# Attention on one core: the causal mask of a diagonal piece added by one product over 128 rows in place of two over 64

## What is computed

```python
q = (x @ wq.T).reshape(B, S, N_HEADS, HEAD_DIM)      # B 4, S 2048, 16 heads of 16
k = (x @ wk.T).reshape(B, S, N_KV_HEADS, HEAD_DIM)   # 4 heads of keys and values
v = (x @ wv.T).reshape(B, S, N_KV_HEADS, HEAD_DIM)
attn = jnp.einsum('bqhd,bkhd->bhqk', q, k) * scale   # k, v repeated for 4 query heads each
causal = jnp.tril(jnp.ones((S, S), dtype=bool))
attn = jnp.where(causal, attn, jnp.float32(-jnp.inf))
attn = jax.nn.softmax(attn, axis=-1)
out = jnp.einsum('bhqk,bkhd->bqhd', attn, v).reshape(B, S, C)
```

## Time and profile before

| what | value |
|---|---|
| median of three executions | 8469.42 us |
| the three executions | 8474.6, 8468.7, 8469.42 us |
| span of the profiled execution, first to last instruction | 8471.3 us |
| TensorE busy in it | 7608.0 us, 90% of the span |
| VectorE busy | 7340.3 us, 87% |
| ScalarE busy | 5072.8 us, 60% |
| GpSimd busy | 3704.5 us, 44% |
| first and last mask product (both attentions) | 203.9 and 7929.3 us |

### The profile page before, as it was taken

One profiled execution on the slowest core, in us unless ns is written; L12 is line 12 of the kernel. 1 busy time (PEld: TensorE's weight loads), 2 busy tenths in 40 slices (PEclk: granted clock), 3 DMA queues, 4 the chain that ended last, 5 costly groups with the idle time before them and its releaser, 6 DMA issues. The chain is left out here.

```text
span 8471.3 us, 131822 instructions
## 1 busy us (share of the span) xinstructions
PE 7608.0 (90%) x38817; PEld 3068.7 (36%) x38818; DVE 7340.3 (87%) x10750; ACT 5072.8 (60%) x7665; POOL 3704.5 (44%) x1825
## 2 busy tenths in 40 slices
PE   6999999989987888888888888888889999999899
PEld 3333333325542333333333333333453333333355
DVE  6988888858877999999999999999658888888588
ACT  3577777762255666666665556556316777777622
POOL 0010011100016999999999999999400000110000
PEclk9899999989998999999999999999988999999999
DMA  6001101112262222222233333333561001010121
GB/s 177 18 19 20 19 19 19 20 37 70 67 232 91 85 83 83 84 83 83 83 98 103 100 100 100 101 103 97 164 181 18 19 19 19 19 22 18 36 78 61
DMA packets 531283, 603.88 MB, mean 71 GB/s; under 512 B 195488, under 2 KB 344736, under 8 KB 526560
## 3 DMA queue, kind: packets, MB, share of 16 engines
q1 hardware_dynamic: 526048, 562.63, 22.4%
q0 software_dynamic: 4608, 33.56, 2.0%
HBM read 397.75 MB, written 163.69 MB: 66 GB/s over the span
## 5 line engine op out<-in xcount | busy, mean ns | idle before, releaser
L833 DVE TENSOR_REDUCE ffn_att_mx<-psum 128x1 f32<-128x512 f32 (+3 forms) x4608 | 2728.0, 654 | 367.8 <-PE psum L674 209.2
L794 ACT ACTIVATE ffn_att_e<-psum,unscale 128x1024 f32<-128x1024 f32 (+3 forms) x2560 | 2376.5, 985 | 766.3 <-PE psum L739 760.3
L1707 POOL TENSOR_TENSOR scan_h<-scan_h,scan_cs 128x1024 f32<-128x1024 f32 x1024 | 2412.4, 2449 | 203.8 <-ACT scan_state L1878 198.0
L1788 PE MATMUL psum<-scan_h,ident 128*128 128x512 f32 x4096 | 1977.7, 624 | 158.9 <-POOL scan_h L1707 157.6
L2022 DVE TENSOR_TENSOR_SCAN scan_h<-psum,scan_state,scan_db 128x512 f32<-128x512 f32 x1408 | 1684.6, 1261 | 10.5 <-ACT psum L1920 10.5
L641 POOL TENSOR_SCALAR_AFFINE_SELECT ffn_att_e<-ffn_att_e 128x512 f32<-128x512 f32 x512 | 324.6, 634 | 3023.9 <-ACT ffn_att_e L794 3023.9
L674 PE MATMUL psum<-ffn_att_k,ffn_att_q 48*128 48x512 f16 (+3 forms) x5120 | 1438.8, 367 | 175.4 <-DMA ffn_att_v<-v 55.8
L1788 PEld LDWEIGHTS psum<-scan_h,ident 128*128 128x128 f32 x4096 | 777.7, 198 | 1321.1 <-issue 894.5
L705 PE MATMUL psum<-ffn_att_e,ffn_att_v 128*32 128x512 f32 (+3 forms) x10240 | 1240.4, 557 | 7.8 <-ACT ffn_att_o L809 2.4
L1920 ACT ACTIVATE psum<-scan_dt,scan_anr 128x512 f32<-128x512 f32 x1024 | 698.2, 682 | 460.2 <-DVE scan_h L2022 459.4
L674 PEld LDWEIGHTS psum<-ffn_att_k,ffn_att_q 48*128 48x128 f16 x5120 | 394.8, 94 | 1559.4 <-DVE ffn_att_mx L833 1260.7
(11 more groups left out here) (256 smaller groups left out, 7118.0 us busy)
## 6 DMA issues: line engine op xcount, KB each, us to landing
scan_cs<-scan_bcd SPq DMA_DIRECT2D x520, 256.0 KB, 3.2
scan_bs<-scan_bcd SPq DMA_DIRECT2D x162, 256.0 KB, 3.4
scan_win<-xp SPq DMA_DIRECT2D x34, 1036.0 KB, 7.0
scan_dt<-scan_sp POOLq DMA_DIRECT2D x32, 1024.0 KB, 7.0
mamba_out_ffn_in_ys<-yz SPq DMA_DIRECT2D x18, 1024.0 KB, 7.6
scan_yi<-y SPq DMA_DIRECT2D x17, 1024.0 KB, 6.7
ffn_att_q<-q_parts SPq DMA_DIRECT2D x128, 128.0 KB, 2.8
ao<-ffn_att_on SPq DMA_DIRECT2D x128, 128.0 KB
```

What stands on the lines that cost most here:

```text
L794: nc.scalar.activation(E[:, s % PB, 2 * hp:2 * hp + 2, off:CH], psum[:, 2 * hp:2 * hp + 2, off:CH], ACT.Exp, scale=unscale[:, 0:1]).then_i ...
L833: nc.vector.reduce_max(mx[:, hh * 2 + pairs[0]:hh * 2 + pairs[1], i // HALF, i % HALF, c // TT], psum[:, turn, 0:(pairs[1] - pairs[0]) * w ...
L1707: nc.gpsimd.tensor_tensor(hh, hh, cs[:, n % NCS, :].unsqueeze(1).to_broadcast([P, 2, CH]), ALU.mult).then_inc(hc_ready, 1)
L1788: ins = nc.tensor.matmul(psum[:, m, :], ident[:, :], h[n % NH][:, m, :], start=False, stop=n == DS - 1)
```

## The change

`mask` and `pick` lose their three copies: each is one 128 by 128 matrix, the triangle and the identity. The mask of a diagonal piece is added by one product over all 128 rows, without a `tile_position`, in place of two over the 64 rows of the piece. The number of mask products falls from 4096 to 2048 in the whole kernel. The product of queries and keys before it stays in its half of the rows. Nothing else is moved.

```diff
-        mask = sb("mask", [P, 3, P], BF16)
-        pick = sb("pick", [P, 3, P], BF16)
+        mask = sb("mask", [P, P], BF16)
+        pick = sb("pick", [P, P], BF16)
...
-                nc.gpsimd.affine_select(out=mask[:, :, :], in_=mask[:, :, :], compare_op=ALU.is_ge, fill=NEG, base=-ROWS,
-                                        pattern=[[ROWS, 3], [-1, P]], channel_multiplier=1).then_inc(made, 1)
-                nc.gpsimd.affine_select(out=pick[:, :, :], in_=pick[:, :, :], compare_op=ALU.not_equal, fill=1.0, base=-ROWS,
-                                        pattern=[[ROWS, 3], [-1, P]], channel_multiplier=1).then_inc(made, 1)
+                nc.gpsimd.affine_select(out=mask[:, :], in_=mask[:, :], compare_op=ALU.is_ge, fill=NEG, base=0,
+                                        pattern=[[-1, P]], channel_multiplier=1).then_inc(made, 1)
+                nc.gpsimd.affine_select(out=pick[:, :], in_=pick[:, :], compare_op=ALU.not_equal, fill=1.0, base=0,
+                                        pattern=[[-1, P]], channel_multiplier=1).then_inc(made, 1)
...
-                    at, rows_at = slice(hh * ROWS, hh * ROWS + PARTS), slice(hh * ROWS, (hh + 1) * ROWS)
+                    at = slice(hh * ROWS, hh * ROWS + PARTS)
...
-                        for z in range(2 * is_diag):
-                            ins = nc.tensor.matmul(psum[:, turn, (j + 1) * w - P:(j + 1) * w], pick[rows_at, 1 - hh + z, :],
-                                                   mask[rows_at, 1 - hh + z, :], start=False, stop=z == 1, tile_position=(hh * ROWS, 0))
+                        if is_diag:
+                            ins = nc.tensor.matmul(psum[:, turn, (j + 1) * w - P:(j + 1) * w], pick[:, :], mask[:, :], start=False, stop=True)
...
-                nc.vector.memset(mask[:, :, :], 0.0).then_inc(made, 1)
-                nc.vector.memset(pick[:, :, :], 0.0).then_inc(made, 1)
+                nc.vector.memset(mask[:, :], 0.0).then_inc(made, 1)
+                nc.vector.memset(pick[:, :], 0.0).then_inc(made, 1)
```

## The result

The changed kernel takes 8771.88 us, the median of four executions (8742.56 to 8795.26), against 8469.06 for the one before (four, 8465.47 to 8474.6): a ratio of 1.0359, 95% interval 1.034 to 1.0378. It is slower by 303 us, where 210 were forecast, and lies 22 us above the top of the range. The profiled execution is the slowest of the four, with a span of 8793.5 us against 8471.3: 322 us more.

The account below looks back on a forecast made before the run. VectorE was taken as mostly the bound, TensorE as the chain in steps with diagonal pieces. Terms: 195 (iterations) + 1 (last iterations) + 16 (pieces ahead) − 2 (start) = 210 us, giving 8680 us; range 8590 to 8750.

Parts of the forecast that it names:

- The price of a switch: Each head of a diagonal piece: changing the array's division costs 0.10 us in and 0.09 out, as for the transpose.
- The steps at full clock: Attention iterations, summed step by step: 6.5 us more in each, 195 us over 30 iterations.
- 8 to 11: Steps with diagonal pieces, on a TensorE chain that no other engine covers: 3.0 us more an iteration.
- step 24: Step of an iteration, followed by roomy steps: 0.2 us more.
- The run-in: 116 pieces ahead of each attention, at half clock: 40 diagonal ones outrun VectorE, 8 us each time, 16 in all.
- The clock is granted in full, 1.00, in all these rows: Said of the profile's windows by step, from iteration 5; no size given.
- Added, first: Diagonal pairs: the 128-row product needs both halves, so the two pieces follow one another; no size of its own.
- The rival with a free switch: Diagonal pieces: the switch costs nothing, only the overlap goes; 36 us more, 8506 us; chance 0.08.
- Not slower: Rival, steps 8 to 11, 15, 21, 34, 37: pairs already serial, no drain; −36 us, 8434 us; chance 0.04.
- TensorE has room: In the attention VectorE is mostly the later engine: TensorE's L674 weight loads wait 541.8 us for it in 1380.
- Catching up: TensorE regains time in steps 12 and 13, −0.4 us; in every VectorE-bound step, 4.5 us an iteration, 8605 us.
- The strict order: Matmuls start and end in program order, so no overlap to lose: 0.14 us a head, 5.3 an iteration, near 8645.

Follow-up runs that it names:

- e7: The changed kernel with L674 of diagonal pieces also over all 128 rows, without tile position, and Q cleared by GpSimd: 8453.9 us, ratio 0.9984.
- e4: The kernel before with L674 of ordinary pieces issued twice in steps without diagonal pieces where VectorE seems the bound: 8520.4 us, ratio 1.0063.
- e3: The changed kernel with L674 of ordinary pieces issued twice in steps without diagonal pieces where VectorE seems the bound: 8814.53 us, ratio 1.0404.
- e11: The kernel before with the second mask product cut to 64 columns and L674 issued twice in step 5 alone: 8408.02 us, ratio 0.9932.
- e6: The changed kernel with L674 of the two-headed diagonal pieces issued twice, same result: 8981.42 us, ratio 1.0602.
- e9: The kernel before with the 128-row mask product only for pieces 0 to 11, those of steps 8 to 11: 8555.38 us, ratio 1.0101.
- e10: The kernel before with the 128-row mask product for every diagonal piece but those of steps 8 to 11: 8592.82 us, ratio 1.0146.
- e1: The changed kernel with L674 of diagonal pieces also over all 128 rows, without tile position, and Q cleared by VectorE: 8505.58 us, ratio 1.0049.

## Why the prediction was wrong

**The price of a switch: right.** 0.32 us from L674 to its mask and a head of width + 0.27, as taken from the transpose in the earlier trace rows: 0.10 us beyond the last column on the way in and 0.10 on the way out (0.16 from mask to L674, of which 0.05 is columns and 0.01 start). The Trainium skill's rule that a change of tiling mode drains TensorE ("TensorEngine Tiling (Array Packing)", Key Properties) agrees with these 0.10 us, and with e7, where they are gone.

**The steps at full clock: right, 7.1 for 6.5 us.** Steps 3 and 4 have +0.65 (0.6 forecast), 8 to 11 +2.6 (3.0), 12 and 13 −0.1 (−0.4), 15 +0.52 (0.55), 34 +0.32 and 21 +0.34 (0.35 each), 18 and 30 with what the steps behind give back +0.6 (0.6), 37 +0.86 (0.8), 7, 16 and 27 with theirs +0.6 (0.45). One term was mis-sized: step 24, +0.74 for 0.2. It has two D256 pieces last, at 0.75 us each against VectorE's 0.6, and step 25 gives nothing back. That they empty VectorE's queue there is my reading; no run takes it apart.

**The run-in: right**, 7.8 us each for 8.

**The step that failed is that no term stood for the clock.** "The clock is granted in full, 1.00, in all these rows" was true of iteration 5, from which all rows came, and not of its neighbours: the same trace has 187 us at half clock in 30 iterations, and only 4 of them without any. The sum took that amount as fixed. It became 465 us: eight spells now began in step 8, where none had, two from step 5 lasted 34 us in place of at most 14, and steps 8 to 11 take 19.18 us in place of 11.58 then. In the profiled execution, 112 us above what the sum gives for it (8793.5 for 8682), that is 99 us, and the steps at full clock have 18 more, 7.1 for 6.5, less some 5 elsewhere. The executions with the higher mean clock, 0.944, are the shorter ones (8743 and 8766 us, against 8778 at 0.940 and 8795 at 0.937), so the clock also goes with most of the spread, which grew from 9 to 53 us. The range left the clock out as well: its upper end, 8746, was made of steps at full clock alone, though "a changed clock" stood among the signs of being wrong.

**Attribution.** "Added, first", that the pieces of a pair follow one another, was argued from a true observation, and costs 0.17 to 0.34 us in steps 3, 9, 10 and 11, but with the saved product beside it only 0.1 us an iteration (e7). The sum was not hurt, as it was made from whole steps. The rival with a free switch, 8506 us, was put too high for the same reason: e7, its nearest case, took 8454, and had +0.1 us an iteration where the rival had 1.2. "Not slower" fell by the 0.32 us. "TensorE has room", read from 541.8 us of waits for banks, was wrong in the sense in which I used it: e4 puts 0.21 us more into such steps and most of them grow by 0.22. Catching up was there in steps 12, 17, 19, 28 and 31, 0.2 to 0.55 us each, all of them right behind steps that the change had made longer.

**The strict order** that the Trainium skill gives for matmuls ("TensorE: Matmul & The Clock Gate", The mechanism) would have given 8645 us. The trace disagrees for row-tiled products in two halves, by the two L674 that take 0.40 us ahead of the first mask. The measured time is no evidence either way: e7 has no overlap, and an iteration of it is 0.1 us longer.

What stays open: what in these stretches makes the granted clock fall. Second products in ordinary pieces raised it (e3, e4, e11), second products among the switches lowered it (e6), and the long spells were there with switches in steps 8 to 11 and not without (e9, e10). No run separates the emptied array from the longer stretch.

## What to carry to other kernels

Count how often consecutive matmuls change the division of the array (rows, columns or none): each trip there and back cost 0.2 us here on TensorE's chain, and 0.11 to 0.13 as a mean over the iteration, more than the product that it saved, and two small products in the same division are cheaper than one in another. Before trusting a stage's rows, look at the granted clock over all iterations of it, not in the cleanest one, and give the clock a term of its own wherever the change lowers or stretches what TensorE does. A VectorE busy for all of a step may still have a TensorE chain right behind it (e4, +0.22 us in step 31).

## What the runs showed of the hardware that was not expected

- Products in the two halves of the rows did not keep the program's order here: at 799.57 us L674 of hh = 1 starts 0.01 us after that of hh = 0 and 0.22 us before the masks of hh = 0 that stand ahead of it in the program; so two L674s take 0.40 us.
- Half a clock does not double the time: 278 us more at half clock cost 99 us, where a doubling would have made it 139. In steps 8 to 11, where TensorE is the chain, it is 7.6 us on 11.6.
- A harmless second issue of six products in step 5 (0.3 us) brought half-clock time from 152 to 68 us and made the kernel faster by 28 us, 8436 to 8408.
- 37 us more in the last stage, with six stalls of VectorE, came with e1 and went with e7, though nothing there had been changed. Small differences of whole kernels are only worth reading stage by stage.
